# One attention loop of a fused four-stage kernel: the shared turning bank is read one step sooner, and the delta gain moves from the tanh's scale into the queries and two sums

## The chip, the cores and the metric

One core of a Trainium2 chip runs the whole program. The metric is the device time of one execution in microseconds, the median of several runs. A step, here, is one pass of the attention loop described below.

## The reference

The function is two transformer layers on an input of 2 x 1024 rows of 128 numbers (the arrays are batched as 4 x 256 or 2 x 1024 in the source; the kernel treats them as `BATCH, SEQ = 2, 1024`). Each of four stages is `x = x + layernorm(stage(layernorm(x)))`: a causal attention with rotary positions (stage a), a ternary feed-forward (b), a differential cosine attention (c), a mixture of eight experts (d). The change lies in stage c, which computes for each of 2 x 8 heads:

```
q1, q2, k1, k2 = halves of q and k, 8 numbers each
cos_scale = 15 * sigmoid(raw) * (1 + 0.5 * tanh(head_delta - mean))
L1 = l2norm(q1) . l2norm(k1) * cos_scale
L2 = l2norm(q2) . l2norm(k2) * cos_scale
G  = tanh(delta_gain * (L1 - L2))
A1 = softmax(L1 + G)
A2 = softmax(L2 - G)
attn = A1 - lambda * A2
y  = attn @ v, then an rms norm per head, then @ Wo.T + bo
```

## The kernel before

The program is written engine by engine in one block, and every dependence is a semaphore wait written out by hand. An engine does its instructions in the order of its own text; a wait holds all that stands behind it on that engine.

**The attention loop of stage c.** There are `NH = 16` heads (two batches of eight) and in each `BT = 8` tiles of 128 keys, so 128 steps, numbered s = 8n + mt. The text below writes (n, mt) for a step. Scores are kept transposed, keys on partitions, 1024 queries on columns. PSUM has eight banks of 512 columns. Banks 0 and 1 hold L1 - L2, banks 2 and 3 hold L1, banks 4 and 5 hold -L2 (the second half of the keys carries a minus, so that one product over both halves gives L1 - L2), bank 6 holds the head's accumulators (four groups of 32 rows, one for each softmax and half of the queries), and bank 7 is the *turning bank* that everything else in this phase shares.

In step s the engines do the following.

- ScalarE: the tanh of step s+2 (`tanh_step`, line 838; the scale is the head's gain, read per partition from the tile `gain`), then the exponential of step s, 2048 columns for both softmaxes (line 868), which waits for both sums of step s.
- VectorE: two sums (`z_step`, lines 1131 and 1134), L1 + G, and then -1 times banks 4 and 5 less G, which is L2 - G, into the tile `hid`. The first waits for the tanh, for the exponential two steps back, which frees the tile, and for the product L1; the second waits for the product L2.
- TensorE: the difference product of step s+3 (line 590), a turn through bank 7 if this step has one (`c_turning`), the product L1 of step s+2, the value products of step s (line 609, 8 instructions, which wait for the exponential of step s), the product L2 of step s+2. In a head's first step the value products also wait until the accumulators of the head before have been read.
- GpSimd: builds the spread query and key operands of the head after the next (`build_qk`), the values (`build_v`), and copies the head's gain into `gain`, one element per partition, from `gains`.

**What goes through the turning bank.** `turning(n, mt)` names the use of a step: the next head's keys at mt 0 and queries at mt 2, the output of the head before at mt 4, late pieces of earlier work at mt 6 in heads 0 to 3, and a few special ones in heads 9 to 14 (the table `SPECIAL`: outputs of the first batch turned, multiplied with Wo, turned again, routed). In heads 10 and 12 nearly every step has one. TensorE may write the bank only when the use before has been read:

```
pe.wait_ge(S["turn_read"], turns_done(use) - 1)
```

VectorE reads it in `turn_out`, which waits until TensorE has turned. In VectorE's loop this read stands two steps late, and the accumulators of the head before are read at mt 1:

```
z_step(n * BT + mt, mt)
use = turning(*divmod(n * BT + mt - 2, BT)) if n * BT + mt >= 2 else None
if use:
    turn_out(use)
if mt == 1 and n:
    acc_out(n - 1)
```

`acc_out` waits for all eight value products of that head. Behind these come, at steps named one by one, small pieces of other work on VectorE: statistics, Newton steps, routing.

**The table of factors.** `c_table`, called once on VectorE during stage b, makes `cs_tab` out of the head's cosine scale; it is multiplied into the inverse norms: the queries get the cosine scale, the keys 1 and -1. The kernel's last part is the driver, which only lays out inputs.

Of the kernel before, what the change touches and what calls it, by code (L numbers as in the profile page):

```python
# [20 lines left out]
ALU = mybir.AluOpType  # L21
# [3 lines left out]
P = 128  # L25
# [106 lines left out]
def sandwich(nc, x_in, a_w, rope, b_w12, b_h1, b_h2, b_w3, b_s, b_s3, c_w, c_wo, c_bo, small,  # L132
             d_wg, d_wu, d_wd, d_wr, ident_in, ident_bf_in, mask_in, before_in, out):
    with ExitStack() as ctx:
# [3 lines left out]
        def sem(name):  # L138
# [67 lines left out]
        v_h = sb("v_h", [P, 2, BT, VW])  # L206
        gain = sb("gain", [P, 2])
        gg = [probs[:, 0], probs[:, 1]]
# [34 lines left out]
        y_2 = [y[:], rot[:, 0].rearrange("p (a b) -> p a b", a=CT)]  # L243
        gains = sb("gains", [P, BATCH * HEADS])

# [12 lines left out]
            small_c fact_c  # L258
            uq uk vh gcp turned turn_read crossed dd l1 l2 g z1 z2 e av accout
            ro to_a ms_o yc ytp yt wo wo_read xn_d tp_d xt_d rt_d z_d tanh_d dist_d ex_d  # L260
# [26 lines left out]
        def c_table(dve, v, me):  # L287

            dve.wait_ge(S["fact_c"], 1)

            me.step(v.tensor_tensor(tiny[:, 48:49], tiny[:, 1:2], tiny[:, 0:1], ALU.subtract))
            me.mark(v.tensor_scalar(nlam[:], tiny[:, 48:49], -LAMBDA_INIT, None, ALU.add))

            me.mark(v.tensor_scalar(tiny[:, 49:50], tiny[:, 16:17], COS_MAX / 2, COS_MAX / 2, ALU.mult, ALU.add))
            me.step(v.tensor_scalar(tiny[:, 8:16], tiny[:, 8:16], 0.5, 1.0, ALU.mult, ALU.add))
            me.step(v.tensor_scalar(tiny[:, 8:16], tiny[:, 8:16], tiny[:, 49:50], None, ALU.mult))
            me.mark(v.tensor_copy(cs_tab[:, 0].rearrange("p h k c -> p h (k c)"),
                                  tiny[:, 8:16].unsqueeze(2).to_broadcast([P, HEADS, 2 * CT])))
            me.mark(v.memset(cs_tab[:, 1, :, :, 0], 1.0))
            me.step(v.memset(cs_tab[:, 1, :, :, 1], -1.0))  # L300
# [430 lines left out]
        def _(act):  # L731
# [102 lines left out]
            def tanh_step(s, u, mt):  # L834
                act.wait_ge(S["dd"], s + 1)
                if s >= 3:
                    act.wait_ge(S["z2"], s - 2)
                A(gg[s % 3], banks[:, 0:2 * CHUNK], ACT.Tanh, scale=gain[:, u:u + 1]).then_inc(S["g"], 1)  # L838

# [13 lines left out]

            act.wait_ge(S["gcp"], 1)
            for mt in range(2):
                tanh_step(mt, 0, mt)
            for n in range(NH):
                for mt in range(BT):
                    s = n * BT + mt
                    if s + 2 < NH * BT:  # L860
                        n2, mt2 = divmod(s + 2, BT)
                        if mt2 == 0:
                            act.wait_ge(S["gcp"], n2 + 1)
                        tanh_step(s + 2, n2 % 2, mt2)
# [43 lines left out]
        def _(dve):  # L908
# [216 lines left out]

            def z_step(s, mt):
                dve.wait_ge(S["g"], s + 1)
                if s >= 2:
                    dve.wait_ge(S["e"], s - 1)
                dve.wait_ge(S["l1"], s + 1)  # L1130
                v.tensor_tensor(zz[:, mt % 2, 0:SEQ], banks[:, 2 * CHUNK:4 * CHUNK], gg[s % 3],  # L1131
                                ALU.add).then_inc(S["z1"], 1)
                dve.wait_ge(S["l2"], s + 1)
                v.scalar_tensor_tensor(zz[:, mt % 2, SEQ:2 * SEQ], banks[:, 4 * CHUNK:6 * CHUNK], -1.0,  # L1134
                                       gg[s % 3], ALU.mult, ALU.subtract).then_inc(S["z2"], 1)
# [158 lines left out]
            for n in range(NH):  # L1294
                u = n % 2
                for mt in range(BT):
                    at = (n, mt)
                    z_step(n * BT + mt, mt)

                    use = turning(*divmod(n * BT + mt - 2, BT)) if n * BT + mt >= 2 else None  # L1300
                    if use:
                        turn_out(use)
                    if mt == 1 and n:
                        acc_out(n - 1)
# [29 lines left out]
                    if at in ((11, 1), (11, 5)):  # L1334
                        c = mt // 4
                        dve.wait_ge(S["x_c"], c + 1)
                        stats("d_in", c, x_of(c))
                    if at == (12, 4):
                        dve.wait_ge(ld["dw"], 80)
                        me.step(v.reciprocal(rs1[:, 3, 0:1], sm[:, SM_TEMP:SM_TEMP + 1]))  # L1340
# [119 lines left out]
        def _(pool):  # L1460
# [57 lines left out]
            def build_v(n):  # L1518
                u = n % 2
                if n >= 2:  # L1520
                    pool.wait_ge(S["g"], BT * (n - 1))
                g.tensor_scalar(gain[:, u:u + 1], gains[:, n:n + 1], 1.0, None, ALU.mult).then_inc(S["gcp"], 1)
                if n >= 2:
                    pool.wait_ge(S["av"], BT * (n - 1))
                g.tensor_scalar(v_h[:, u, :, 0:VH], v_c[:, n, :, :], 1.0, None, ALU.mult).then_inc(S["vh"], 1)

            rstd_of("b_in", 1)
            pool.wait_ge(ld["cw"], 64)
            for b in range(BATCH):
                me.step(g.tensor_scalar(gains[:, b * HEADS:(b + 1) * HEADS], sm[:, SM_GAIN:SM_GAIN + HEADS],  # L1530
                                        1.0, None, ALU.mult))
            for c in range(1, CHUNKS):
# [170 lines left out]
```

## Time and profile before

| | us |
|---|---|
| median of 3 runs | 791.54 (789.84 to 792.03) |
| the profiled execution, its time | 789.3 |
| the profiled execution, its span | 787.5 |
| first tanh of the attention loop starts | 268.3 |
| last exponential of the loop starts | 670.21 |
| steps of the loop | 128 |

The span is the time from the first to the last recorded instruction, so the execution's own time is 1.8 us longer. Rows of the timeline give the start in us, the length in us, the engine, the line of the kernel, the instruction, the tiles written and read with their shapes, and in brackets how long the engine had stood idle before it and what ended that. DVE is VectorE, ACT ScalarE, PE TensorE's products, PEld its weight loads, POOL GpSimd. A busy time counts instructions from start to end; two neighbours on VectorE or ScalarE overlap a little, so the distance between their starts is less than the length of one. The name `w` in a VectorE row is the tile `acc_sb` where the line is 1180, `hid` is where the sums go, `w_hh` where the exponentials go, and `probs` and `qkv_a` are the three buffers of the tanh.

### The profile page before, as it was taken

To read this page: it belongs to the slowest core of one execution; us is meant where nothing else is said; L and a number is where in the kernel's file an instruction comes from. 1 tells how busy PE (TensorE), PEld (TensorE's weight loads), DVE (VectorE), ACT (ScalarE), POOL (GpSimd) and SP (SyncE) were. 2 spreads that over 40 slices of the span, in tenths; PEclk is the share of its full clock that TensorE was granted. 3 is DMA by queue.
4 is the path that set the end of the run, shared out by engine and by line. 5 is a ranking of instruction groups with operands and counts; after the bars stand their busy time and mean duration, and the time that the engine had idled before them with its cause. 6 is when DMAs were issued, how large, how long until landed. Compare 5 with 4: busy or idle time off the path is not lost.

```text
span 787.5 us, 9791 instructions
## 1 busy us (share of the span) xinstructions
PE 667.7 (85%) x3514; PEld 285.0 (36%) x3514; DVE 565.1 (72%) x1087; ACT 480.9 (61%) x468; POOL 227.9 (29%) x359
## 2 busy tenths in 40 slices
PE   5999899999999578888888888867778776979796
PEld 2576545454544222222222222122222221456364
DVE  4656431507152599999999999979968999768656
ACT  1254323233433279999999999877968998312311
POOL 3601100101013566322339336345713012011001
PEclk9999999999999779999999999999999999999899
DMA  8000200000000110101111100110010013300340
GB/s 298 0 2 0 83 1 0 1 0 1 0 1 0 27 27 14 27 15 28 27 27 27 24 18 18 24 28 10 18 27 15 14 27 108 108 1 14 69 161 27
DMA packets 16753, 26.01 MB, mean 33 GB/s; under 512 B 2496, under 2 KB 7360, under 8 KB 16320
## 3 DMA queue, kind: packets, MB, share of 16 engines
q1 hardware_dynamic: 16704, 25.38, 11.7%
q8 instruction: 28, 0.46, 0.2%
q14 instruction: 21, 0.17, 0.1%
HBM read 15.87 MB, written 1.11 MB: 22 GB/s over the span
## 4 chain that ended last, share of the span: by engine, by line
PE 44%; DVE 28%; ACT 17%; issue 10%; DMA 1%; POOL 0%; SPq 0%; POOLq 0%; DVEq 0%; ACTq 0%
ACT w_hh L868 13%; DVE hid L1131 8%; DVE hid L1134 7%; PE ps L513 7%; PE ps L523 7%; PE ps L621 4%; PE ps L609 4%; PE ps L500 3%; PE ps L590 3%; PE ps L630 3%; PE ps L533 2%; PE ps L420 2%; PE ps L451 2%; ACT probs L838 1%; PE ps L373 1%
## 5 line engine op out<-in xcount | busy, mean ns | idle before, releaser
L868 ACT ACTIVATE w_hh<-hid 128x2048 f32<-128x2048 f32 x128 | 248.4, 1941 | 13.4 <-DVE hid L1134 12.8
L590 PE MATMUL ps<-q_s,k_s 128*128 128x512 bf16 (+1 forms) x512 | 171.3, 399 | 30.3 <-DVE hid L1131 24.9
L609 PE MATMUL ps<-w_hh,v_h 128*32 128x512 f32 x1024 | 140.4, 620 | 32.2 <-ACT w_hh L868 17.9
L838 ACT ACTIVATE probs<-ps,gain 128x1024 f32<-128x1024 f32 x86 | 98.4, 1144 | 28.4 <-PE ps L590 27.1
L1131 DVE TENSOR_TENSOR hid<-ps,probs 128x1024 f32<-128x1024 f32 x86 | 104.6, 1217 | 14.3 <-PE ps L590 9.4
L1134 DVE SCALAR_TENSOR_TENSOR hid<-ps,probs 128x1024 f32<-128x1024 f32 x86 | 104.7, 1217 | 5.3 <-PE ps L590 4.8
L590 PE MATMUL ps<-q_w,k_w 64*128 64x512 bf16 x256 | 102.0, 399 | 0.5 <-DVE hid L1134 0.5
L1468 POOL TENSOR_SCALAR rs<-mv 128x4 f32<-128x4 f32 x32 | 7.3, 229 | 259.9 <-DVE mv L947 259.7
L590 PEld LDWEIGHTS ps<-q_s,k_s 128*128 128x128 bf16 (+1 forms) x512 | 38.4, 95 | 104.5 <-issue 57.2
L1040 DVE SCALAR_TENSOR_TENSOR hid<-ps,s_b,rot 128x512 f32<-128x512 f32 x16 | 11.9, 750 | 87.1 <-ACT rot L811 87.1
L590 PEld LDWEIGHTS ps<-q_w,k_w 64*128 64x128 bf16 x256 | 23.7, 93 | 110.4 <-issue 58.6
L894 ACT ACTIVATE u_q<-ps 128x512 f32<-128x512 f32 x32 | 19.1, 597 | 68.1 <-PE ps L621 68.0
L1131 DVE TENSOR_TENSOR hid<-ps,qkv_a 128x1024 f32<-128x1024 f32 x42 | 51.1, 1216 | 7.0 <-PE ps L590 4.7
L513 PE MATMUL ps<-hid,w_hh 128*128 128x512 f32 x128 | 56.0, 595 | 0.0
L523 PE MATMUL ps<-hid,w_hh 128*128 128x512 f32 x128 | 55.6, 592 | 0.0
L1134 DVE SCALAR_TENSOR_TENSOR hid<-ps,qkv_a 128x1024 f32<-128x1024 f32 x42 | 51.2, 1218 | 4.5 <-PE ps L590 4.3
L838 ACT ACTIVATE qkv_a<-ps,gain 128x1024 f32<-128x1024 f32 x42 | 48.0, 1143 | 7.6 <-PE ps L590 6.8
L1506 POOL TENSOR_SCALAR u_k<-part 128x128 bf16<-128x128 bf16 x96 | 48.0, 528 | 9.7 <-DVE part L1096 9.7
L1506 POOL TENSOR_SCALAR u_q<-part 128x128 bf16<-128x128 bf16 x96 | 47.9, 527 | 0.0
L609 PEld LDWEIGHTS ps<-w_hh,v_h 128*32 128x32 f32 x1024 | 20.8, 109 | 68.1 <-ACT w_hh L868 42.1
L513 PEld LDWEIGHTS ps<-hid,w_hh 128*128 128x128 f32 x128 | 24.0, 190 | 31.7 <-issue 29.4
L816 ACT ACTIVATE hid<-ps,s_b 128x512 f32<-128x512 f32 x16 | 11.0, 687 | 39.5 <-PE ps L513 39.5
(252 smaller groups left out, 994.3 us busy)
## 6 DMA issues: line engine op xcount, KB each, us to landing
k_w<-k_s SPq DMA_DIRECT2D x32, 128.0 KB, 2.3
q_w<-q_s SPq DMA_DIRECT2D x32, 128.0 KB, 2.3
w_hh<-w_rows SPq DMA_DIRECT2D x4, 1024.0 KB, 9.6
w_hh<-in_b_h SPq DMA_DIRECT2D x2, 1024.0 KB, 8.7
hid<-w_rows SPq DMA_DIRECT2D x2, 1024.0 KB, 6.0
part<-w_rows SPq DMA_DIRECT2D x8, 256.0 KB, 7.2
x_res<-in_x SPq DMA_DIRECT2D x4, 256.0 KB, 5.6
tab<-in_rope SPq DMA_DIRECT2D x1, 1024.0 KB, 6.5
```

What stands on the lines that cost most here:

```text
L500: last = mm(ps[:, 2 * (m % 2) + w, :], w_12[:, w, m * P:(m + 1) * P], xt[:], start=True, stop=True)
L513: last = mm(ps[:, o, :], w_h1[:, k, o * P:(o + 1) * P], hid[:, 0, k, :], start=(k == 0), stop=(k == KT_ - 1))
L523: last = mm(ps[:, o, :], w_h2[:, k, o * P:(o + 1) * P], hid[:, 1, k, :], start=(k == 0), stop=(k == KT_ - 1))
L590: last = mm(ps[:, base + half, :], k_op[rows, u, keys], q_op[rows, u, half * CHUNK:(half + 1) * CHUNK], start=True, stop=True)
L609: last = mm(ps[VW * g4:VW * g4 + VW, 6, :], v_h[:, u, mt, :], ee[:, mt % 2, g4 * CHUNK:(g4 + 1) * CHUNK], start=(mt == 0), stop=(mt == BT ...
L621: last = mm(ps[:, 2 * (n % 2) + w, :], wt[:, e, :], xt_d[c], start=True, stop=True)
L630: last = mm(ps[:, 4 + c % 2, k * P:(k + 1) * P], h_d[m % SLOTS][:, k * P:(k + 1) * P], w_d[:, e, :], start=(e == 0 and k == 0), stop=(e == ...
L838: A(gg[s % 3], banks[:, 0:2 * CHUNK], ACT.Tanh, scale=gain[:, u:u + 1]).then_inc(S["g"], 1)
L868: A(ee[:, mt % 2, :], zz[:, mt % 2, :], ACT.Exp).then_inc(S["e"], 1)
L1131: v.tensor_tensor(zz[:, mt % 2, 0:SEQ], banks[:, 2 * CHUNK:4 * CHUNK], gg[s % 3], ALU.add).then_inc(S["z1"], 1)
L1134: v.scalar_tensor_tensor(zz[:, mt % 2, SEQ:2 * SEQ], banks[:, 4 * CHUNK:6 * CHUNK], -1.0, gg[s % 3], ALU.mult, ALU.subtract).then_inc(S["z ...
L1506: last = g.tensor_scalar(out_ap, in_ap, 1.0, None, ALU.mult)
```

## The change

1. The turning bank is read one step sooner: `turn_out` for the use of step s now stands behind the sums of step s+1, not s+2.
2. The accumulators of head n-1 are read at (n, 0), behind the sums of that step, not at (n, 1).
3. The gain goes into the queries: `c_table` multiplies the head's cosine scale with the gain (kept away from zero and infinity by `GAIN_LOW` and `GAIN_HIGH`, sign kept), so all three products come out as gain times the old ones. The tanh then takes no scale. The sums need the old ones back and multiply with the gain's inverse, `gain_inv`, one column for each head and sign: the first sum is no longer a plain addition of two tensors but a scalar_tensor_tensor with a factor read per partition, and the second one's constant -1 becomes such a factor. `c_table` has eight small instructions more.
4. GpSimd no longer copies gains, neither once at the start nor in each head, and ScalarE no longer waits for those copies.
5. The reciprocal of the routing temperature moves from (12, 4) to (11, 3), because the first routing read comes a step sooner.

```diff
 SM_W = 51
+GAIN_LOW, GAIN_HIGH = 1e-20, 1e20
...
         v_h = sb("v_h", [P, 2, BT, VW])
-        gain = sb("gain", [P, 2])
+        gain_inv = sb("gain_inv", [P, 2, HEADS])
         gg = [probs[:, 0], probs[:, 1]]
...
         y_2 = [y[:], rot[:, 0].rearrange("p (a b) -> p a b", a=CT)]
-        gains = sb("gains", [P, BATCH * HEADS])
...
             small_c fact_c
-            uq uk vh gcp turned turn_read crossed dd l1 l2 g z1 z2 e av accout
+            uq uk vh turned turn_read crossed dd l1 l2 g z1 z2 e av accout
             ro to_a ms_o yc ytp yt wo wo_read xn_d tp_d xt_d rt_d z_d tanh_d dist_d ex_d
...
             me.step(v.tensor_scalar(tiny[:, 8:16], tiny[:, 8:16], tiny[:, 49:50], None, ALU.mult))
+            gain = sm[:, SM_GAIN:SM_GAIN + HEADS]
+            me.step(v.scalar_tensor_tensor(tiny[:, 24:32], gain, -1.0, gain, ALU.mult, ALU.max))
+            me.mark(v.tensor_scalar(tiny[:, 24:32], tiny[:, 24:32], GAIN_LOW, GAIN_HIGH, ALU.max, ALU.min))
+            me.step(v.tensor_scalar(tiny[:, 32:40], gain, 0.0, None, ALU.is_ge))
+            me.step(v.tensor_scalar(tiny[:, 32:40], tiny[:, 32:40], 2.0, -1.0, ALU.mult, ALU.add))
+            me.step(v.tensor_tensor(tiny[:, 24:32], tiny[:, 24:32], tiny[:, 32:40], ALU.mult))
+            me.mark(v.tensor_tensor(tiny[:, 8:16], tiny[:, 8:16], tiny[:, 24:32], ALU.mult))
+            me.step(v.reciprocal(gain_inv[:, 0], tiny[:, 24:32]))
+            me.mark(v.tensor_scalar(gain_inv[:, 1], gain_inv[:, 0], -1.0, None, ALU.mult))
             me.mark(v.tensor_copy(cs_tab[:, 0].rearrange("p h k c -> p h (k c)"),
...
                     act.wait_ge(S["z2"], s - 2)
-                A(gg[s % 3], banks[:, 0:2 * CHUNK], ACT.Tanh, scale=gain[:, u:u + 1]).then_inc(S["g"], 1)
+                A(gg[s % 3], banks[:, 0:2 * CHUNK], ACT.Tanh).then_inc(S["g"], 1)
...
-            act.wait_ge(S["gcp"], 1)
             for mt in range(2):
...
                         n2, mt2 = divmod(s + 2, BT)
-                        if mt2 == 0:
-                            act.wait_ge(S["gcp"], n2 + 1)
                         tanh_step(s + 2, n2 % 2, mt2)
...
-            def z_step(s, mt):
+            def z_step(s, h, mt):
                 dve.wait_ge(S["g"], s + 1)
                 dve.wait_ge(S["l1"], s + 1)
-                v.tensor_tensor(zz[:, mt % 2, 0:SEQ], banks[:, 2 * CHUNK:4 * CHUNK], gg[s % 3],
-                                ALU.add).then_inc(S["z1"], 1)
+                v.scalar_tensor_tensor(zz[:, mt % 2, 0:SEQ], banks[:, 2 * CHUNK:4 * CHUNK], gain_inv[:, 0, h:h + 1],
+                                       gg[s % 3], ALU.mult, ALU.add).then_inc(S["z1"], 1)
                 dve.wait_ge(S["l2"], s + 1)
-                v.scalar_tensor_tensor(zz[:, mt % 2, SEQ:2 * SEQ], banks[:, 4 * CHUNK:6 * CHUNK], -1.0,
+                v.scalar_tensor_tensor(zz[:, mt % 2, SEQ:2 * SEQ], banks[:, 4 * CHUNK:6 * CHUNK],
+                                       gain_inv[:, 1, h:h + 1],
                                        gg[s % 3], ALU.mult, ALU.subtract).then_inc(S["z2"], 1)
...
                     at = (n, mt)
-                    z_step(n * BT + mt, mt)
-
-                    use = turning(*divmod(n * BT + mt - 2, BT)) if n * BT + mt >= 2 else None
+                    z_step(n * BT + mt, n % HEADS, mt)
+
+                    use = turning(*divmod(n * BT + mt - 1, BT)) if n * BT + mt else None
                     if use:
                         turn_out(use)
-                    if mt == 1 and n:
+                    if mt == 0 and n:
                         acc_out(n - 1)
...
                         stats("d_in", c, x_of(c))
-                    if at == (12, 4):
+                    if at == (11, 3):
                         dve.wait_ge(ld["dw"], 80)
...
                 if n >= 2:
-                    pool.wait_ge(S["g"], BT * (n - 1))
-                g.tensor_scalar(gain[:, u:u + 1], gains[:, n:n + 1], 1.0, None, ALU.mult).then_inc(S["gcp"], 1)
-                if n >= 2:
                     pool.wait_ge(S["av"], BT * (n - 1))
             rstd_of("b_in", 1)
-            pool.wait_ge(ld["cw"], 64)
-            for b in range(BATCH):
-                me.step(g.tensor_scalar(gains[:, b * HEADS:(b + 1) * HEADS], sm[:, SM_GAIN:SM_GAIN + HEADS],
-                                        1.0, None, ALU.mult))
             for c in range(1, CHUNKS):
```

VectorE's instructions around the border of heads 7 and 8, the sums of step 64 first; `w<-ps` at lines 1180 and 1187 is the read of head 7's accumulators and `k_s<-ps` the read of the turned keys. Before:

```order
464 L1131 TENSOR_TENSOR hid<-ps,probs 128x1024 [waits e_l1,e_e,e_g]
465 L1134 SCALAR_TENSOR_TENSOR hid<-ps,probs 128x1024 [waits e_l2]
466 L1131 TENSOR_TENSOR hid<-ps,qkv_a 128x1024 [waits e_l1,e_e,e_g]
467 L1134 SCALAR_TENSOR_TENSOR hid<-ps,qkv_a 128x1024 [waits e_l2]
468 L1180 COPY w<-ps 128x512 [waits e_turned,e_av]
469 L1131 TENSOR_TENSOR hid<-ps,probs 128x1024 [waits e_l1,e_e,e_g]
470 L1134 SCALAR_TENSOR_TENSOR hid<-ps,probs 128x1024 [waits e_l2]
471 L1143 COPY k_s<-ps 128x1024 [waits e_turned]
```

and in the change:

```order
472 L1137 SCALAR_TENSOR_TENSOR hid<-ps,gain_inv,probs 128x1024 [waits e_l1,e_e,e_g]
473 L1140 SCALAR_TENSOR_TENSOR hid<-ps,gain_inv,probs 128x1024 [waits e_l2]
474 L1187 COPY w<-ps 128x512 [waits e_turned,e_av]
475 L1137 SCALAR_TENSOR_TENSOR hid<-ps,gain_inv,qkv_a 128x1024 [waits e_l1,e_e,e_g]
476 L1140 SCALAR_TENSOR_TENSOR hid<-ps,gain_inv,qkv_a 128x1024 [waits e_l2]
477 L1150 COPY k_s<-ps 128x1024 [waits e_turned]
478 L1137 SCALAR_TENSOR_TENSOR hid<-ps,gain_inv,probs 128x1024 [waits e_l1,e_e,e_g]
479 L1140 SCALAR_TENSOR_TENSOR hid<-ps,gain_inv,probs 128x1024 [waits e_l2]
```

The read of the accumulators stood behind the sums of step 65 and stands behind those of step 64; the keys were read behind the sums of step 66 and are read behind those of step 65.

The same engine in head 10, where almost every step turns something; `y<-ps,b_o` is the read of the first chunk's product with Wo. Before, from the sums of step 82:

```order
527 L1131 TENSOR_TENSOR hid<-ps,probs 128x1024 [waits e_l1,e_e,e_g]
528 L1134 SCALAR_TENSOR_TENSOR hid<-ps,probs 128x1024 [waits e_l2]
529 L1143 COPY k_s<-ps 128x1024 [waits e_turned]
530 L1131 TENSOR_TENSOR hid<-ps,qkv_a 128x1024 [waits e_l1,e_e,e_g]
531 L1134 SCALAR_TENSOR_TENSOR hid<-ps,qkv_a 128x1024 [waits e_l2]
532 L1162 TENSOR_TENSOR y<-ps,b_o 128x512 [waits e_turned]
533 L1131 TENSOR_TENSOR hid<-ps,probs 128x1024 [waits e_l1,e_e,e_g]
534 L1134 SCALAR_TENSOR_TENSOR hid<-ps,probs 128x1024 [waits e_l2]
535 L1145 COPY q_s<-ps 128x1024 [waits e_turned]
```

and in the change, from the sums of step 81:

```order
533 L1137 SCALAR_TENSOR_TENSOR hid<-ps,gain_inv,probs 128x1024 [waits e_l1,e_e,e_g]
534 L1140 SCALAR_TENSOR_TENSOR hid<-ps,gain_inv,probs 128x1024 [waits e_l2]
535 L1150 COPY k_s<-ps 128x1024 [waits e_turned]
536 L1137 SCALAR_TENSOR_TENSOR hid<-ps,gain_inv,probs 128x1024 [waits e_l1,e_e,e_g]
537 L1140 SCALAR_TENSOR_TENSOR hid<-ps,gain_inv,probs 128x1024 [waits e_l2]
538 L1169 TENSOR_TENSOR y<-ps,b_o 128x512 [waits e_turned]
539 L1137 SCALAR_TENSOR_TENSOR hid<-ps,gain_inv,qkv_a 128x1024 [waits e_l1,e_e,e_g]
540 L1140 SCALAR_TENSOR_TENSOR hid<-ps,gain_inv,qkv_a 128x1024 [waits e_l2]
541 L1152 COPY q_s<-ps 128x1024 [waits e_turned]
```

Keys, Wo product and queries are each read one pair of sums sooner; between two reads there is one pair of sums as before.

## Rows read from the trace of the kernel before

**Rows 1.** The page's busy time by engine: busy us, share of the span, instructions.

```profile
PE 667.7 (85%) x3514; PEld 285.0 (36%) x3514; DVE 565.1 (72%) x1087; ACT 480.9 (61%) x468; POOL 227.9 (29%) x359
```

**Rows 2.** Busy time by stretch, cut at exponentials; columns: stretch, length, PE, PEld, DVE, ACT, POOL, clock, DMA.

```profile
301.00:368.15 67.15, 59.53 (x406) 17.02 (x402) 63.83 (x67) 67.15 (x50) 20.98 (x45) 1.00 0.11 25
368.15:437.09 68.94, 58.11 (x400) 15.92 (x396) 66.87 (x77) 67.94 (x50) 33.61 (x48) 1.00 0.11 24
437.09:482.13 45.04, 38.51 (x268) 10.61 (x264) 42.37 (x46) 44.98 (x33) 15.26 (x30) 1.00 0.11 24
482.13:507.75 25.62, 20.87 (x136) 5.40 (x132) 24.73 (x35) 22.88 (x17) 15.57 (x23) 0.93 0.10 21
507.75:538.66 30.91, 22.75 (x160) 7.87 (x156) 24.49 (x32) 23.08 (x18) 12.37 (x21) 1.00 0.08 18
538.66:564.36 25.70, 20.03 (x140) 5.71 (x136) 24.42 (x46) 23.03 (x18) 21.12 (x33) 1.00 0.10 22
564.36:596.30 31.94, 24.69 (x152) 7.63 (x152) 22.88 (x26) 23.04 (x17) 6.69 (x14) 0.89 0.08 17
596.30:619.63 23.33, 19.92 (x140) 5.32 (x132) 22.28 (x29) 23.02 (x20) 6.67 (x14) 1.00 0.11 24
619.63:645.73 26.10, 19.51 (x137) 5.42 (x133) 25.59 (x41) 22.98 (x17) 0.53 (x1) 1.00 0.09 21
645.73:670.21 24.48, 17.41 (x115) 4.16 (x112) 23.39 (x37) 21.07 (x15) 8.56 (x10) 1.00 0.29 88
```

**Rows 3.** Timeline around the border of heads 7 and 8, ScalarE, VectorE and TensorE.

```profile
459.46 1.99 ACT L868 ACTIVATE w_hh<-hid 128x2048 f32<-128x2048 f32 x1
...
460.13 1.22 DVE L1134 SCALAR_TENSOR_TENSOR hid<-ps,probs 128x1024 f32<-128x1024 f32 x1 [0.17 <-PE ps L590]
...
461.50 1.07 PE L609 MATMUL ps<-w_hh,v_h 128*32 128x512 f32 x8 [0.56 <-ACT w_hh L868]
461.54 1.22 DVE L1131 TENSOR_TENSOR hid<-ps,qkv_a 128x1024 f32<-128x1024 f32 x1 [0.18 <-ACT w_hh L868]
...
462.93 1.23 DVE L1134 SCALAR_TENSOR_TENSOR hid<-ps,qkv_a 128x1024 f32<-128x1024 f32 x1 [0.17 <-PE ps L590]
...
463.26 0.61 PE L546 MATMUL ps<-ident_bf,u_k 128*128 128x128 bf16 x8
...
464.06 1.20 ACT L838 ACTIVATE probs<-ps,gain 128x1024 f32<-128x1024 f32 x1
464.07 0.68 DVE L1180 COPY w<-ps 128x512 f32<-128x512 f32 x1
...
465.05 2.00 ACT L868 ACTIVATE w_hh<-hid 128x2048 f32<-128x2048 f32 x1
```

**Rows 4.** Timeline in head 10, VectorE and TensorE around two turns.

```profile
521.17 0.68 DVE L1162 TENSOR_TENSOR y<-ps,b_o 128x512 f32<-128x512 f32 x1
...
521.91 0.62 PE L546 MATMUL ps<-ident_bf,u_q 128*128 128x128 bf16 x8 [1.38 <-DVE y L1162]
...
522.99 1.23 DVE L1131 TENSOR_TENSOR hid<-ps,probs 128x1024 f32<-128x1024 f32 x1 [1.14 <-PE ps L590]
...
525.35 0.68 DVE L1145 COPY q_s<-ps 128x1024 bf16<-128x1024 bf16 x1
```

**Rows 5.** Groups by form; columns: instruction, shapes, count, busy us, mean ns, idle before.

```profile
L894 ACT ACTIVATE u_q<-ps 128x512 f32<-128x512 f32 x32 | 19.1, 597 | 68.1 <-PE ps L621 68.0
...
L1040 DVE SCALAR_TENSOR_TENSOR hid<-ps,s_b,rot 128x512 f32<-128x512 f32 x16 | 11.9, 750 | 87.1 <-ACT rot L811 87.1
...
L811 ACT ACTIVATE rot<-ps,s_b 128x512 f32<-128x512 f32 x16 | 10.9, 687 | 22.0 <-PE ps L500 22.0
...
L1045 DVE TENSOR_TENSOR y<-ps,s 128x512 f32<-128x512 f32 x4 | 2.7, 683 | 15.4 <-PE ps L533 15.4
```

**Rows 6.** Timeline of stage b: the normalised tile written, and turned.

```profile
148.97 1.11 DVE L954 TENSOR_SCALAR xn_c<-x_res,mv,rs 128x128 f32<-128x128 f32 x4 [0.58 <-POOL rs L1469]
...
166.16 0.60 PE L373 MATMUL ps<-ident,xn_c 128*128 128x128 f32 x4
```

## The prediction

> **What bounds the kernel now.** The first view, busy time by engine, only says that no engine is full over the whole span: TensorE 85%, VectorE 72%, ScalarE 61% [rows 1]. The change acts in the second attention, a loop of 16 heads times 8 key tiles, 128 steps. So I read a table by stretch next, cut where one exponential of a head's last step starts and the same one of a later head starts: heads 1 to 3, 4 to 6, 7 and 8, then 9 to 15 one by one [rows 2]. Two kinds of stretch show. In heads 1 to 8 ScalarE is busy all the time (67.15 of 67.15 us in heads 1 to 3) and a head takes 22.4 us, 2.80 a step. In heads 9 to 15 ScalarE has holes, and heads 10 and 12 take 30.91 and 31.94 us although VectorE is busy for only 24.49 and 22.88 of them.
>
> The timeline explains both. In a plain head, one step of ScalarE is a tanh and an exponential, each starting when the one before ends: from the exponential at 459.46 to the one two steps later at 465.05 are 5.59 us, and tanh to exponential is 0.99 [rows 3]. VectorE's second sum at 462.93 lasts 1.23 and the next instruction starts 1.14 after it, so neighbours overlap by 0.08; two sums make 2.27 a step, a copy of 0.68 makes 0.60, and there is slack. In a crowded head there is a turn of data through the last PSUM bank in every step, and it is serial: VectorE reads the bank at 521.17, only then comes TensorE's next turn at 521.91 after 1.38 us of waiting, then the product, then VectorE's next sum at 522.99 after 1.14 of waiting, and the next read at 525.35 [rows 4]. That makes steps of 4.2 us.
>
> **The change, part by part.**
>
> *The bank is read one step sooner.* TensorE's turn of step s waits for the read of the turn of step s-1. That read stood behind the sums of step s+1 and now stands behind those of step s, which are over when TensorE gets there. The loop of rows 4 opens: the turn runs beside VectorE's next sums. What is left of a crowded head is the work of VectorE. Head 10: 24.49 busy, less some 0.4 of instruction tails that only stand out beside a gap, plus 1.07 for the new factor (below), plus 0.3 of waiting: 25.4, so **-5.5 us**. Head 12: VectorE has 22.88 - 0.7 + 1.07 = 23.2, ScalarE 22.8 (a plain head, below), and one late copy in its first steps: 23.4, **-8.5 us**; a part of its excess is TensorE's clock, granted at a mean of 0.89 here, between its levels of 1.2 and 2.4 GHz, and at 1.00 in heads 10 and 11 [rows 2]; TensorE is idle for 7 of this stretch's 32 us, and I don't cost the clock apart.
>
> *The accumulators are read one step sooner too.* This is the part that costs. They need the value products of the head's last step, which need that step's exponential. Rows 3, counted from that exponential's start (459.46 = 0): value products at 2.04, lasting 1.07, so the read can start at about 3.18. VectorE is through with the next step's sums at 0.67 + 1.14 = 1.8, with the new factor and the shorter ScalarE step at 1.95. Before, it went on with the next sum at 2.08; now it stands for 1.2 us, copies for 0.60, and starts that sum at 3.78. The second sum follows at 4.98 and its exponential 1.31 after that (1.24 now, by the 462.93 sum's own length, and the factor's 0.07), at 6.29; ScalarE would have been ready at 5.40. Loss 0.89. The key copy follows directly and costs 0.30 more; after that VectorE catches up. So a head's border costs **1.2 us** where ScalarE bounds.
>
> *The tanh takes no factor.* Activations of 512 columns take 687 ns with a factor read per partition and 597 without [rows 5], so 0.09 less, and neighbours overlap by 0.1 in both forms. A ScalarE step falls from 2.80 to 2.70. A plain head becomes 8 x 2.70 + 1.2 = 22.8 against 22.4: the gain of 0.7 is more than eaten. Heads 1 to 3 +1.3, heads 7 and 8 +1.2 (with the reciprocals of step (8,6)).
>
> *The sums multiply with a factor read per partition.* The trace has no such sum of 1024 columns. At 512, with one PSUM input, it takes 750 ns with the factor and 683 without [rows 5]; bounds are 0 and 0.07, and I take 0.067, since it is the same engine, memory and operation, and the difference should be a fixed piece. Two sums per step make 0.13, and 1.07 per head where VectorE bounds.
>
 The factorless row (683) agrees, the 750 row doesn't fit; by the rule alone the sum would be that of the first rival.
>
> *Where VectorE bounds or nearly does*, the new length is its busy time [rows 2] plus 1.07 a head plus the border wait (0.9 to 1.2, or 0.3 where it comes late by itself). Heads 4 to 6: 66.87 + 3.2 + 0.9 = 71.0, +2.1. Head 9: 24.73 + 1.07 + 1.2 = 27.0, +1.4. Head 11: 24.42 + 1.07 + 0.9 = 26.4, +0.7. Head 13: 22.28 + 1.07 + 0.9 = 24.3, +1.0. Head 14: 25.59 + 1.07 + 0.3 = 27.0, +0.9. Head 15: 23.39 + 1.07 + 0.3 = 24.8, +0.3. Head 0 pays the factor only: +0.8.
>
> *Costed at nothing.* The eight small instructions in the table of factors: VectorE's chain there ends in the normalised tile, done at 150.08, which TensorE turns at 166.16 [rows 6]; some 2 us of small work fit in the gap, and were they not covered they would cost these 2 us. GpSimd's copies of the gain (0.2 us a head) go, beside work it waits with anyway. The reciprocal moved from (12,4) to (11,3) is 0.15 in either place.
>
> **Sum.** Gains 5.5 + 8.5 = 14.0. Losses 0.8 + 1.3 + 2.1 + 1.2 + 1.4 + 0.7 + 1.0 + 0.9 + 0.3 = 9.7. Net -4.3 us. The profiled execution took 789.3 (span 787.5), so 785.0; it lies 2.2 below the median of 791.5, against which I forecast **787.2 us**. A measurement of this kernel can tell about 0.3%, 2.4 us, from no change.
>
> **Rivals.**
> 1. *The factor is free on VectorE* at 1024 columns, its fetch covered by the instruction before. For: two instructions in a row overlap already. Against: so they do around the 750 ns row. Then 1.07 drops out of the seven heads 9 to 15 (in head 12 only 0.3) and of head 0 (7.8 us), a plain border costs 0.9 instead of 1.2 (-1.5 over five), heads 4 to 6 give 1: -10 more, 777. Chance 0.12.
> 2. *The tanh's saving doesn't reach its neighbour*: its factor is fetched beside the exponential before it, so the start-to-start time stays 0.99 and the step 2.80. Borders then cost 0.9 and a plain head is 23.3, +0.5 over eight heads: about 791, no change. Chance 0.14.
> 3. *Slower: the border wait isn't absorbed at all.* The place is the read of the accumulators. If TensorE's products behind it also come late, as after today's read (the sum at 462.93 already waited for its product), VectorE's whole 1.2 + 0.6 us arrive at ScalarE in each of 15 heads, instead of 1.2: +9 us, net +4.7, 796. It decides from 1.2 + 4.3/15 = 1.5 us a border. For: VectorE has only 0.3 us of slack a step left to recover with. Against: the next products need only a sum and an exponential that are early. Chance 0.15.
>
> That the early reads find their turn not ready, so that VectorE waits in plain steps, is a small thing by the same rows: the turn at 463.26 is over at 463.87, 1.6 us after its step's exponential started (halfway between 459.46 and 465.05), and VectorE comes at about 1.95.
>
> **Numbers.** The forecast has 0.52, with a range of its own of 782 to 792; about three quarters of it are faster by over 2.4 us. With rival 1, faster is 0.54; with rival 2 and the forecast's edge, same is 0.27; with rival 3 and remains, slower is 0.19. The range that should hold 8 in 10, 779.5 to 795.5, leaves out most of rival 1 and half of rival 3.
>
> **What would show it.** Right: steps of 4.2 us gone in heads 10 and 12, which take 25.4 and 23.4; the tanh at about 1.05 us and plain steps of 2.70; both sums at 1.28; a wait of about 1.2 us of VectorE for the value products before each accumulator copy, some 15 times; plain heads of 22.8. Wrong: sums still at 1.22 (rival 1), plain steps of 2.80 with a shorter tanh (rival 2), plain heads above 23.2 (rival 3), or crowded heads that keep waits of TensorE for reads of the bank.

## The result, and the profile after

The changed kernel takes **784.14 us** (783.85 to 784.7, 4 runs) beside 790.83 us of the kernel before (789.84 to 792.03, 4 runs): a ratio of 0.9916, 95% interval 0.9898 to 0.9933, so about 6.6 us less. The profiled executions stand closer, 782.9 us of span against 787.5, since that of before lay 1.5 us under its median and that of the changed kernel 0.6 over. The tables below go by the profiled ones.

The page's busy time by engine, of the changed kernel, which answers to [rows 1]:

```profile
PE 664.6 (85%) x3514; PEld 285.5 (36%) x3514; DVE 576.4 (74%) x1095; ACT 471.4 (60%) x468; POOL 224.1 (29%) x341
```

VectorE has 11.3 us more work, ScalarE 9.5 us less. The same table by stretch as [rows 2], cut at the same exponentials (those that end heads 0, 3, 6, 8, 9, 10, 11, 12, 13, 14 and 15); columns are stretch, length, PE, PEld, DVE, ACT, POOL, clock, DMA:

```profile
301.30:369.52 68.22, 60.05 (x410) 16.93 (x402) 65.48 (x67) 65.74 (x49) 19.96 (x41) 1.00 0.11 24
369.52:440.66 71.14, 59.73 (x404) 15.90 (x396) 69.15 (x75) 66.28 (x49) 32.99 (x45) 0.98 0.10 23
440.66:486.66 46.00, 38.92 (x268) 10.55 (x264) 43.47 (x46) 43.97 (x33) 15.16 (x29) 1.00 0.11 24
486.66:513.27 26.61, 19.44 (x136) 5.29 (x132) 25.48 (x35) 22.37 (x16) 15.04 (x21) 1.00 0.09 20
513.27:538.27 25.00, 21.82 (x160) 8.39 (x156) 24.49 (x33) 22.37 (x17) 12.13 (x20) 1.00 0.10 22
538.27:564.63 26.36, 21.31 (x140) 5.86 (x136) 25.48 (x47) 22.36 (x17) 20.92 (x32) 0.94 0.09 21
564.63:587.90 23.27, 21.25 (x156) 7.86 (x152) 22.52 (x24) 22.13 (x16) 6.47 (x13) 1.00 0.11 23
587.90:612.07 24.17, 19.38 (x136) 5.26 (x132) 22.96 (x29) 22.47 (x21) 6.45 (x13) 1.00 0.11 24
612.07:640.68 28.61, 21.00 (x137) 5.79 (x133) 26.93 (x41) 22.48 (x18) 0.53 (x1) 0.94 0.09 19
640.68:665.82 25.14, 17.35 (x115) 3.92 (x111) 24.36 (x37) 20.53 (x16) 8.57 (x10) 1.00 0.28 85
```

| heads | before | after | moved | forecast |
|---|---|---|---|---|
| 0 | 25.05 | 25.14 | +0.1 | +0.8 |
| 1 to 3 | 67.15 | 68.22 | +1.1 | +1.3 |
| 4 to 6 | 68.94 | 71.14 | +2.2 | +2.1 |
| 7, 8 | 45.04 | 46.00 | +1.0 | +1.2 |
| 9 | 25.62 | 26.61 | +1.0 | +1.4 |
| 10 | 30.91 | 25.00 | -5.9 | -5.5 |
| 11 | 25.70 | 26.36 | +0.7 | +0.7 |
| 12 | 31.94 | 23.27 | -8.7 | -8.5 |
| 13 | 23.33 | 24.17 | +0.8 | +1.0 |
| 14 | 26.10 | 28.61 | +2.5 | +0.9 |
| 15 | 24.48 | 25.14 | +0.7 | +0.3 |

From the loop's last exponential to the end are 117.1 us now and 117.3 before, so the loop makes the whole difference. Two heads give 14.6 us, and the other fourteen take 10.0 of them back.

The crowded head. Timeline of the changed kernel in head 10, VectorE alone, where [rows 4] showed it standing still between two reads of the turning bank:

```profile
519.35 0.68 DVE L1150 COPY k_s<-ps 128x1024 bf16<-128x1024 bf16 x1
519.94 1.28 DVE L1137 SCALAR_TENSOR_TENSOR hid<-ps,gain_inv,probs 128x1024 f32<-128x1024 f32 x1
521.13 1.28 DVE L1140 SCALAR_TENSOR_TENSOR hid<-ps,gain_inv,probs 128x1024 f32<-128x1024 f32 x1
522.33 0.69 DVE L1169 TENSOR_TENSOR y<-ps,b_o 128x512 f32<-128x512 f32 x1
522.92 1.28 DVE L1137 SCALAR_TENSOR_TENSOR hid<-ps,gain_inv,qkv_a 128x1024 f32<-128x1024 f32 x1
524.11 1.28 DVE L1140 SCALAR_TENSOR_TENSOR hid<-ps,gain_inv,qkv_a 128x1024 f32<-128x1024 f32 x1
525.30 0.69 DVE L1152 COPY q_s<-ps 128x1024 bf16<-128x1024 bf16 x1
```

Sum, sum, read, sum, sum, read, with no idle time in brackets: 2.98 us from one read to the next (519.35, 522.33, 525.30) instead of 4.18. VectorE is busy for 24.49 of the head's 25.00 us; it is the bound.

The border. Timeline of the changed kernel around heads 7 and 8, all engines, which answers to [rows 3]:

```profile
463.41 1.93 ACT L874 ACTIVATE w_hh<-hid 128x2048 f32<-128x2048 f32 x1
...
464.11 1.28 DVE L1140 SCALAR_TENSOR_TENSOR hid<-ps,gain_inv,probs 128x1024 f32<-128x1024 f32 x1
...
465.39 1.07 PE L618 MATMUL ps<-w_hh,v_h 128*32 128x512 f32 x8 [0.46 <-ACT w_hh L874]
...
466.52 0.69 DVE L1187 COPY w<-ps 128x512 f32<-128x512 f32 x1 [1.13 <-PE ps L618]
...
467.13 1.28 DVE L1137 SCALAR_TENSOR_TENSOR hid<-ps,gain_inv,qkv_a 128x1024 f32<-128x1024 f32 x1
...
468.32 1.28 DVE L1140 SCALAR_TENSOR_TENSOR hid<-ps,gain_inv,qkv_a 128x1024 f32<-128x1024 f32 x1
...
469.51 0.68 DVE L1150 COPY k_s<-ps 128x1024 bf16<-128x1024 bf16 x1
469.63 1.91 ACT L874 ACTIVATE w_hh<-hid 128x2048 f32<-128x2048 f32 x1 [0.67 <-DVE hid L1140]
```

From the exponential of head 7's last step (463.41) the value products start at 1.98, VectorE stands for 1.13 us and reads the accumulators at 3.11, the next first sum comes at 3.72 and its exponential at 6.22, after 0.67 us in which ScalarE waits for the sum. The second sum of 464.11 was over early enough to have gone on at about 2. The forecast had 3.18, 3.78 and 6.29. Over the loop this wait is a group of its own; from the chart of who waited for whom (total, times, longest):

```profile
DVE w L1187 <- PE ps L618: 14.1, 16, 3.1
```

Leaving out the last one of 3.1, after the loop, 15 borders make 11.0 us of standing still.

And the two operands, from the page's groups (mean ns of one is the number after the busy time), first two groups of the kernel before and then the same two of the changed one:

```profile
L838 ACT ACTIVATE probs<-ps,gain 128x1024 f32<-128x1024 f32 x86 | 98.4, 1144 | 28.4 <-PE ps L590 27.1
L1131 DVE TENSOR_TENSOR hid<-ps,probs 128x1024 f32<-128x1024 f32 x86 | 104.6, 1217 | 14.3 <-PE ps L590 9.4
...
L1137 DVE SCALAR_TENSOR_TENSOR hid<-ps,gain_inv,probs 128x1024 f32<-128x1024 f32 x86 | 109.9, 1277 | 4.3 <-ACT probs L847 3.9
...
L847 ACT ACTIVATE probs<-ps 128x1024 f32<-128x1024 f32 x86 | 87.5, 1017 | 14.5 <-PE ps L599 14.5
```

The sums went from 1217 to 1277 ns, the tanh from 1144 to 1017.

### The profile page after: what moved, and what is told of

It reads as the page before. It is cut to its first block, busy times and chain, and to the rows that moved or that the text cites. A ratio compares the mean times of both kernels' runs of the same rounds, so it can differ in the third digit from the quotient of the medians.

```text
span 782.9 us, 9779 instructions
## 1 busy us (share of the span) xinstructions
PE 664.6 (85%) x3514; PEld 285.5 (36%) x3514; DVE 576.4 (74%) x1095; ACT 471.4 (60%) x468; POOL 224.1 (29%) x341
## 4 chain that ended last, share of the span: by engine, by line
PE 41%; DVE 34%; ACT 13%; issue 10%; DMA 1%; POOL 0%; SPq 0%; POOLq 0%; DVEq 0%; ACTq 0%
DVE hid L1137 12%; ACT w_hh L874 9%; DVE hid L1140 8%; PE ps L522 7%; PE ps L532 7%; PE ps L630 4%; PE ps L509 3%; PE ps L618 3%; PE ps L639 2%; PE ps L542 2%; PE ps L429 2%; PE ps L460 2%; ACT probs L847 2%; DVE st L950 1%; PE ps L599 1%
## 5 line engine op out<-in xcount | busy, mean ns | idle before, releaser
L874 ACT ACTIVATE w_hh<-hid 128x2048 f32<-128x2048 f32 x128 | 244.7, 1912 | 36.6 <-DVE hid L1140 36.4
L1137 DVE SCALAR_TENSOR_TENSOR hid<-ps,gain_inv,probs 128x1024 f32<-128x1024 f32 x86 | 109.9, 1277 | 4.3 <-ACT probs L847 3.9
L1140 DVE SCALAR_TENSOR_TENSOR hid<-ps,gain_inv,probs 128x1024 f32<-128x1024 f32 x86 | 109.9, 1278 | 0.6 <-PE ps L599 0.3
L847 ACT ACTIVATE probs<-ps 128x1024 f32<-128x1024 f32 x86 | 87.5, 1017 | 14.5 <-PE ps L599 14.5
L1137 DVE SCALAR_TENSOR_TENSOR hid<-ps,gain_inv,qkv_a 128x1024 f32<-128x1024 f32 x42 | 53.6, 1277 | 0.2
L1140 DVE SCALAR_TENSOR_TENSOR hid<-ps,gain_inv,qkv_a 128x1024 f32<-128x1024 f32 x42 | 53.7, 1277 | 0.1
L1529 POOL TENSOR_SCALAR v_h<-v_c 128x128 f32<-128x128 f32 x16 | 8.5, 530 | 140.6 <-PE ps L618 140.6
L847 ACT ACTIVATE qkv_a<-ps 128x1024 f32<-128x1024 f32 x42 | 42.8, 1018 | 3.4 <-PE ps L599 3.4
```

The source lines that it names most:

```text
L847: A(gg[s % 3], banks[:, 0:2 * CHUNK], ACT.Tanh).then_inc(S["g"], 1)
L874: A(ee[:, mt % 2, :], zz[:, mt % 2, :], ACT.Exp).then_inc(S["e"], 1)
L1137: v.scalar_tensor_tensor(zz[:, mt % 2, 0:SEQ], banks[:, 2 * CHUNK:4 * CHUNK], gain_inv[:, 0, h:h + 1], gg[s % 3], ALU.mult, ALU.add).then_ ...
```

## The experiments

The question is which of the three parts (bank read sooner, accumulators read sooner, gain folded) brings and which costs, and whether the border is dear for the reason given. All ratios are to the kernel before, timed on the same chip. The first four runs were timed on one chip and the last four on another, so where two runs across that line are compared, the difference by their ratios stands beside that of the medians.

### The early read of the bank alone

```diff
-                    use = turning(*divmod(n * BT + mt - 2, BT)) if n * BT + mt >= 2 else None
+                    use = turning(*divmod(n * BT + mt - 1, BT)) if n * BT + mt else None
...
-                    if at == (12, 4):
+                    if at == (11, 3):
```

> The kernel before with the turning bank read one step sooner (and the routing reciprocal at (11, 3)), nothing else; the accumulators are still read at (n, 1), behind the key read. My theory: this edit alone carries the gain, and it lacks the border wait and the factor. Head 10 falls from 30.9 to about 24.0 us, head 12 from 31.9 to about 23.0, head 11 by 1, plain heads stay at 22.4: 17 us less, about 774. Rival (the gain comes from the fold of the gain, and the read only moves the waits): heads 10 and 12 stay above 28 us and the time falls by 5 at most.

Measured 775.88 us (775.6 to 776.99), ratio 0.9807 (0.9791 to 0.9823): 15.5 us less, more than twice what the whole change gives. The stretches of heads 10 and 12 of this kernel:

```profile
511.28:535.59 24.31, 21.68 (x160) 8.42 (x156) 23.64 (x33) 22.76 (x18) 12.43 (x21) 1.00 0.10 23
559.99:582.86 22.87, 21.10 (x156) 7.89 (x152) 22.16 (x24) 22.51 (x17) 7.38 (x16) 1.00 0.11 24
```

24.31 and 22.87 against 30.91 and 31.94. The rival, which gave the gain to the fold, falls. What I missed is in the plain heads: they take 22.9, not 22.4, with one long step at each border. Timeline of this kernel there, VectorE and TensorE:

```profile
467.17 0.68 DVE L1143 COPY k_s<-ps 128x1024 bf16<-128x1024 bf16 x1
...
467.76 0.68 DVE L1180 COPY w<-ps 128x512 f32<-128x512 f32 x1
...
468.55 1.07 PE L609 MATMUL ps<-w_hh,v_h 128*32 128x512 f32 x8 [1.26 <-DVE w L1180]
```

With the bank read a step sooner, the key copy and the accumulator copy meet in the same step, keys first. TensorE's value products wait 1.26 us for the accumulators, and with them the second product behind them. TensorE's clock is granted in full (1.00) in both crowded heads of this run, and head 12 had 0.89 before; head 10 had 1.00 already and still fell by 6.6 us, so there the gain can't be the clock's.

### The fold of the gain alone

The changed kernel with both reads put back:

```diff
-                    use = turning(*divmod(n * BT + mt - 1, BT)) if n * BT + mt else None
+                    use = turning(*divmod(n * BT + mt - 2, BT)) if n * BT + mt >= 2 else None
...
-                    if mt == 0 and n:
+                    if mt == 1 and n:
```

> The changed kernel with both reads where they were before, so the fold of the gain alone. My theory: ScalarE's step falls from 2.80 to 2.70, plain heads to 21.6 or 21.7 us (8 heads, about -5), while the serial steps of heads 10 and 12 and the heads that VectorE bounds pay 0.13 us a step (about +2.5): 2 to 3 us less, about 788. Rival (the fold makes the gain): 6 us less or more.

Measured 796.82 us (796.45 to 798.39), ratio 1.0074 (1.0058 to 1.0089): 5 to 6 us *more*. Both theories fall. ScalarE's undisturbed step did become 2.70, but heads 1 to 3 take 22.3 each, since two steps at the border take 3.18 and 2.84; in heads 7 and 8 these steps take 2.87 and 2.85. Timeline of this kernel around the border of heads 7 and 8, VectorE and TensorE:

```profile
466.16 0.68 DVE L1187 COPY w<-ps 128x512 f32<-128x512 f32 x1
...
466.94 1.06 PE L618 MATMUL ps<-w_hh,v_h 128*32 128x512 f32 x8 [0.72 <-DVE w L1187]
...
468.38 1.28 DVE L1140 SCALAR_TENSOR_TENSOR hid<-ps,gain_inv,probs 128x1024 f32<-128x1024 f32 x1 [0.34 <-PE ps L599]
```

The value products wait 0.72 us for the accumulators, the second sum then waits 0.34 for its product. The kernel before has the same two waits at this border:

```profile
464.86 1.07 PE L609 MATMUL ps<-w_hh,v_h 128*32 128x512 f32 x8 [0.66 <-DVE w L1180]
...
466.29 1.22 DVE L1134 SCALAR_TENSOR_TENSOR hid<-ps,probs 128x1024 f32<-128x1024 f32 x1 [0.40 <-PE ps L590]
```

There that lateness is covered by a ScalarE step of 2.80 and sums of 1.22; here the step is shorter and the sums longer, and the cover is gone. The last two runs below bear this out on another base: at the border of heads 7 and 8 the shorter step alone costs 0.12 us and the longer sums alone at most 0.04, both together 0.21. The heads in which VectorE has other work pay as well: heads 4 to 6 +1.7, head 11 +2.4, head 14 +2.1. Of the last two a part may be the clock's: it was 0.88 and 0.94 there in this profiled execution against 1.00 before.

### The early read of the accumulators alone

```diff
-                    if mt == 1 and n:
+                    if mt == 0 and n:
```

> The kernel before with only the read of the accumulators moved to (n, 0). My theory of the border: VectorE stands 1.2 us for the value products, the next exponential is late by about 0.56 us, so plain heads take 22.9 instead of 22.4 and the whole about 5 us more, 796. Rival (in the changed kernel it is the key read right behind that makes a border dear, not the wait): plain heads stay at 22.4, and the time doesn't change.

Measured 795.7 us (794.77 to 803.68), ratio 1.0072 (1.0046 to 1.0099): 4 to 6 us more, where 5 were forecast. Timeline of this kernel at the border of heads 7 and 8, VectorE and ScalarE:

```profile
465.69 0.69 DVE L1180 COPY w<-ps 128x512 f32<-128x512 f32 x1 [1.28 <-PE ps L609]
...
468.67 1.91 ACT L868 ACTIVATE w_hh<-hid 128x2048 f32<-128x2048 f32 x1 [0.37 <-DVE hid L1134]
```

VectorE stands 1.28 us for the value products, ScalarE then 0.37 us for the sum; the step takes 3.31 instead of 2.80, and plain heads 22.9. The key copy is a step away here, so the wait alone makes a border dear, by 0.5 us of the 1.1 that it costs in the changed kernel, and the rival falls. The rest comes with the shorter step, the longer sums and the key copy; no run has these apart at this border. (This profiled execution was 8 us over the kernel's median. Its heads 10 to 12 take 98.6 us against 88.6 before, at granted clocks of 0.86, 0.83 and 0.85 against 1.00, 1.00 and 0.89; only its plain heads are read here.)

The three parts by themselves add up to -15.5 + 5.4 + 4.3 = -5.8 us by the medians, to -3.7 by the ratios, beside the -6.6 of the whole change.

### The changed kernel with the accumulators read at (n, 1) again

```diff
-                    if mt == 0 and n:
+                    if mt == 1 and n:
```

> The changed kernel with the accumulators read at (n, 1) again, behind the key read. My theory: the border of a plain head falls from 1.1 to 0.3 us or less and plain heads to about 21.9; the heads bound by VectorE lose their 0.9 us of waiting but get back some of the wait for the second product: about 10 us less than the changed kernel, 774. Rival (the key read makes the border dear): VectorE now has two copies in a row there, and the time stays at 784 or rises.

Measured 780.87 us (779.53 to 783.03), ratio 0.9875 (0.9856 to 0.9893): 3.3 us under the changed kernel, a third of what I expected. A plain head takes 22.4 with a border step of 3.49, so a border costs 0.8 instead of 1.1. VectorE and TensorE at the border of heads 7 and 8:

```profile
466.46 0.68 DVE L1150 COPY k_s<-ps 128x1024 bf16<-128x1024 bf16 x1
467.06 0.68 DVE L1187 COPY w<-ps 128x512 f32<-128x512 f32 x1
...
467.85 1.06 PE L618 MATMUL ps<-w_hh,v_h 128*32 128x512 f32 x8 [1.32 <-DVE w L1187]
```

The wait for the values is gone, and the meeting of the two copies has come in its place, as in the first run.

This run and the first one differ by the fold alone, on one chip, and both were granted a clock of 1.00 from head 1 on: the fold costs 5.0 us here (780.87 against 775.88). It takes 1.5 us off heads 1 to 3 and 0.6 off heads 7 and 8, and puts 0.6 on head 9, 0.8 on head 10 and 1.1 on each of heads 11, 14 and 15.

### The same, accumulators ahead of the keys

```diff
+                    if mt == 1 and n:
+                        acc_out(n - 1)
                     if use:
                         turn_out(use)
-                    if mt == 0 and n:
-                        acc_out(n - 1)
```

> The changed kernel with the accumulators read at (n, 1), and ahead of the key read. My theory: with the copies the other way round TensorE's value products start 0.6 us sooner, and the second product with them; a border costs 0.3 us instead of the 0.8 of the run with the key read first, plain heads take 21.9 us: about 775. Rival (two copies in a row cost the same in either order): 781, as in that run.

Measured 773.89 us (773.61 to 775.07), ratio 0.9794 (0.978 to 0.9808): 7.0 us under the run before by the medians, 6.4 by the ratios. VectorE and TensorE at the border of heads 7 and 8:

```profile
463.20 0.68 DVE L1187 COPY w<-ps 128x512 f32<-128x512 f32 x1
463.80 0.68 DVE L1150 COPY k_s<-ps 128x1024 bf16<-128x1024 bf16 x1
...
463.98 1.06 PE L618 MATMUL ps<-w_hh,v_h 128*32 128x512 f32 x8 [0.72 <-DVE w L1187]
```

The border step is 2.91 in heads 2 to 4, 7 and 8, a cost of 0.2, and heads 2, 3 and 7 take 21.85; heads 4 and 8 take 23.4 and 22.4, for a long step near their end. The order of two copies of 0.6 us each was worth 6 to 7 us.

### Early read, accumulators first, no fold

```diff
-                    use = turning(*divmod(n * BT + mt - 2, BT)) if n * BT + mt >= 2 else None
+                    use = turning(*divmod(n * BT + mt - 1, BT)) if n * BT + mt else None
+                    if mt == 1 and n:
+                        acc_out(n - 1)
                     if use:
                         turn_out(use)
-                    if mt == 1 and n:
-                        acc_out(n - 1)
```

> The kernel before with the turning bank read one step sooner and, at (n, 1), the accumulators read ahead of the keys; the gain stays the tanh's scale. My theory: as the run with the early read alone (775.9), less its 0.5 us a border: plain heads 22.4, about 769, better than both kernels. Rival: 776.

Measured **770.03 us** (769.28 to 771.17), ratio 0.9741 (0.9727 to 0.9756): the best kernel of this study that computes the reference, 14 us under the changed one and 21 under the one before. Timeline of this kernel at the border, VectorE, TensorE and ScalarE:

```profile
462.31 2.00 ACT L868 ACTIVATE w_hh<-hid 128x2048 f32<-128x2048 f32 x1
...
464.13 0.68 DVE L1180 COPY w<-ps 128x512 f32<-128x512 f32 x1
464.73 0.68 DVE L1143 COPY k_s<-ps 128x1024 bf16<-128x1024 bf16 x1
...
464.91 1.07 PE L609 MATMUL ps<-w_hh,v_h 128*32 128x512 f32 x8 [0.66 <-DVE w L1180]
465.11 2.00 ACT L868 ACTIVATE w_hh<-hid 128x2048 f32<-128x2048 f32 x1
...
467.90 2.01 ACT L868 ACTIVATE w_hh<-hid 128x2048 f32<-128x2048 f32 x1
```

Both copies follow each other, the value products wait 0.66 us only, and ScalarE goes on every 2.80 us: heads 1 to 3 take 67.12 us, as 24 steps of 2.80 do (67.2).

### The tanh's side of the fold by itself

```diff
-                A(gg[s % 3], banks[:, 0:2 * CHUNK], ACT.Tanh, scale=gain[:, u:u + 1]).then_inc(S["g"], 1)
+                A(gg[s % 3], banks[:, 0:2 * CHUNK], ACT.Tanh).then_inc(S["g"], 1)
```

> The run before this one with the tanh's scale left out, so the gain is not applied at all. It gives the tanh's side of the fold by itself. My theory: ScalarE's step 2.70, plain heads 21.7, heads that VectorE bounds unchanged: 6 us less, 763. Rival (VectorE is so close that the saving is lost): 1 or 2 us less.

This kernel leaves out the gain. Measured 764.58 us (764.47 to 765.66), ratio 0.9674 (0.9661 to 0.9687): 5.5 us under its base. Steps of 2.70, heads 1 to 3 65.23 us instead of 67.12; head 9 25.32 against 25.37 and head 10 23.66 against 23.70, where VectorE bounds. At a border the step is 2.82, a cost of 0.12.

### The sums' side of the fold by itself

```diff
-                v.tensor_tensor(zz[:, mt % 2, 0:SEQ], banks[:, 2 * CHUNK:4 * CHUNK], gg[s % 3],
-                                ALU.add).then_inc(S["z1"], 1)
+                v.scalar_tensor_tensor(zz[:, mt % 2, 0:SEQ], banks[:, 2 * CHUNK:4 * CHUNK], gain_inv[:, 0, 0:1],
+                                       gg[s % 3], ALU.mult, ALU.add).then_inc(S["z1"], 1)
...
-                v.scalar_tensor_tensor(zz[:, mt % 2, SEQ:2 * SEQ], banks[:, 4 * CHUNK:6 * CHUNK], -1.0,
+                v.scalar_tensor_tensor(zz[:, mt % 2, SEQ:2 * SEQ], banks[:, 4 * CHUNK:6 * CHUNK], gain_inv[:, 1, 0:1],
```

> The same base (early read, accumulators first) with the tanh's scale kept and both sums multiplying with a factor read per partition, here 1 and -1. It gives the sums' side of the fold by itself. My theory: sums of 1.28 instead of 1.22 us; about 1.07 us more in each head that VectorE bounds (9, 10, 11, 13, 14, 15), little in plain heads: 7 us more, 776. Rival (the factor is hidden behind the wait for the product or the tanh): no change, 769.

Measured 777.82 us (777.12 to 778.29), ratio 0.9838 (0.9824 to 0.9851): 7.8 us over its base. Two groups of this kernel's page, the sums with their factor and the tanh with its own:

```profile
L1134 DVE SCALAR_TENSOR_TENSOR hid<-ps,gain_inv,probs 128x1024 f32<-128x1024 f32 x86 | 109.9, 1278 | 4.6 <-ACT probs L841 3.6
...
L841 ACT ACTIVATE probs<-ps,gain 128x1024 f32<-128x1024 f32 x86 | 97.6, 1134 | 15.7 <-PE ps L593 15.6
```

Heads 1 to 3 stay at 67.19 us; the loss is in head 0 (+1.1), heads 4 to 6 (+1.3), 9 (+0.5), 10 (+0.7), 11 (+1.2), 12 (+0.3), 13 (+0.4), 14 (+1.1) and 15 (+0.8). The clock of this execution was a little lower than that of its base in heads 11 (0.93 against 1.00) and 14 (0.88 against 0.94), so a part of these two may be the clock's; the two runs at a full clock compared above give 1.1 in each, too.

The two sides together: -5.5 + 7.8 = +2.3, and the fold measured whole on this base (773.89 against 770.03) +3.9. Of the 1.6 us that the sum lacks, 1.1 lie in heads 1 to 3, 7 and 8 of the profiled executions, where the whole fold brings 1.9 us and the two sides apart 3.0: there the longer sums eat into what the shorter step saves. In head 0 the whole fold costs 1.5 and the sides 0.7, but its execution had a clock of 0.71 there against 0.80 to 0.86 in the three others. The fold loses, since in half of the heads ScalarE bounds with VectorE close behind it, so little is saved, and in the other half VectorE bounds and pays in full.

## Why the prediction was right

The forecast of 787.2 and the range of 779.5 to 795.5 hold the 784.14, the sign is right, and the size was somewhat short: 4.3 forecast, 4.6 between the profiled executions, 6.6 by the ratio. The forecast was added up on profiled executions, and what makes the medians 2 us further apart than these isn't traced.

- *The bank is read one step sooner.* Right, by mechanism and size: heads 10 and 12 take 25.00 and 23.27 us where 25.4 and 23.4 were forecast, VectorE bounds the first, and the read alone gives 15.5 us. That TensorE's clock, 0.89 in head 12 before, would rise was left uncosted; it is 1.00 there now.
- *The border costs 1.2 us.* Right: three steps of 3.52, 2.98 and 2.72 us at the border of heads 7 and 8, 9.22 instead of 3 x 2.70, so 1.1. The run with this edit alone shows that the wait makes a border dear, with 0.5 us beside a step of 2.80 and sums of 1.22. That here 0.9 of it would be the wait and 0.3 the key copy behind it fits the trace (the first two steps are 0.82 and 0.28 over 2.70, and VectorE goes through sums and key copy without a gap), but no run has the two apart. Plain heads take 22.74, 22.8 forecast. VectorE's wait is 1.13 us in a plain head and 0.7 on the mean of the 15 borders, since it is shorter where VectorE comes late by itself (0.3 in head 14).
- *The tanh takes no factor.* Right: 2.70 a step. The wider picture was short: I valued the fold by itself at 2 to 3 us of gain in the expectations, and it costs 5. The step that failed there is the border of the kernel before, which I took as free at 2.70 as it had been at 2.80, though the waits of 0.66 and 0.40 us around it were in the trace; the prediction itself never needed that border, since the change moves the read.
- *The sums' factor costs 0.067.* The second sum's start-to-start time went from 1.14 to 1.20 and 1.19 (521.13 to 522.33 and 524.11 to 525.30 above) and its length by 60 ns; so 0.06 was paid, near the upper bound, and the first rival, with the factor free, falls.
- *Heads by their VectorE work.* Nine of eleven stretches came within 0.4 us. Head 14 was the miss, +2.5 where +0.9 was forecast: VectorE is busy for 26.93 of its 28.61 us (26.7 forecast), and the rest are small waits of 0.3 to 0.4 us for values, product and turn, where I had allowed one of 0.3. TensorE's clock fell to 0.94 in that stretch, a term that the forecast doesn't have. The other runs show its size: with the fold and a clock of 1.00 (both runs with the accumulators read at (n, 1) behind the early read) the head takes 27.32, and 28.15 at 0.94 in the run of the fold alone; without the fold 26.25 with the early read alone at 1.00, 27.32 in the best kernel at 0.94. So a lower clock went with about 1 us, most of the miss. It doesn't cost in every head: head 9 takes 25.62 us at 0.93 before and 25.77 at 1.00 with the early read. Head 0 was put at +0.8 and moved by 0.1, though VectorE's busy time there grew by 0.7 (24.07 to 24.77); why so little of it shows is open.
- *The costed-at-nothing parts.* The loop's first exponential starts 0.2 us later than before (276.16 against 275.95), and what follows the loop takes the same time.
- The second rival (the tanh's saving doesn't arrive) falls by the steps of 2.70, the third (a border of 1.8) by those of 1.1.

## What to carry to other kernels

A read out of a shared buffer belongs as early as its data is sure to be there, and no earlier: one step sooner opened a serial loop for the bank (-15.5 us), and made a wait for the accumulators (+4 to +6 us), both by one line in the same loop. Where two engines take turns at bounding, moving work from one to the other is priced stretch by stretch, and a busy share says little; here 0.1 us a step off ScalarE and 0.12 onto VectorE made a loss of 4 to 6 us on three different bases (3.9, 5.0, and 5.4 by the medians or 5.9 by the ratio). Of two reads that meet in one step, the one that another engine's next work waits for goes first.

## What the runs showed of the hardware

- A factor read per partition costs time on both engines. A VectorE sum of 1024 columns is recorded 60 ns longer with it (1217 to 1277) and starts the next one 0.05 to 0.06 us later; at 512 columns the difference is 67 ns (683 to 750), so it didn't grow with the width between these two. On ScalarE a step of a tanh and an exponential falls from 2.80 to 2.70 us without it, while the tanh's recorded length falls by 127 ns (1144 to 1017).
- The recorded length of an activation drifts while its rhythm doesn't: at the border rows before, exponentials are recorded with 1.99 and 2.00 us [rows 3], in the changed kernel with 1.93 and, right after a wait, 1.91, though the work is the same. In heads 1 and 2 before, the exponentials' recorded length rises from 1.93 (at 303.80) to 2.03 us (at 345.74), and their starts stay 2.80 apart. So the lengths of ScalarE should be read start to start.
- One exchange of two 0.6 us copies, with the same work on every engine, changed the time by 7.0 us with the fold (780.87 to 773.89) and by 5.9 without (775.88 to 770.03) by the medians, which come from two chips; by the ratios by 6.4 and 5.2.
